# Attention with two decay kernels and a recurrent step: issuing 46 small transfers per batch from GpSimd instead of SyncE

## The reference

```
x = layernorm(x + attention(x))        # x: 16 batches x 512 tokens x 256
x = layernorm(x + ffn(x))              # a gated recurrence over the 16 batches

def attention(x):                      # 16 heads of 16
    q = heads(x @ Wq)
    out_short = softmax(q k_s^T / 4 + decay_bias) v_s     # k_s, v_s from x @ Wkv_short
    out_long  = softmax(q k_l^T / 4) v_l                  # k_l, v_l from x @ Wkv_long
    return (alpha * out_short + (1 - alpha) * out_long) @ Wo
```

## Time and profile before

| | |
|---|---|
| median of 3 executions | 2106.11 us (2104.06 to 2107.74) |
| the profiled execution: time, span | 2103.92 us, 2102.1 us |
| TensorE busy | 2015.2 us, 96% of the span |
| VectorE, ScalarE busy | 1528.0 us (73%), 1454.0 us (69%) |
| GpSimd busy | 257.6 us (12%) |
| DMAs issued by SyncE: `o_att`, `dens`, `inv_dram`, `inverses` | 512, 128, 32, 64 |
| the attention, the recurrence and the output | up to about 1750 us, from there on |

### The profile page before, as it was taken

How to read it: one execution, slowest core, us unless ns; L and a number is a source line. 1 busy time by engine, 2 the same in 40 slices (tenths; PEclk the granted TensorE clock), 3 DMA queues, 4 the chain that set the end, 5 groups by cost and what they waited for, 6 DMA issues and landing times.

```text
span 2102.1 us, 40632 instructions
## 1 busy us (share of the span) xinstructions
PE 2015.2 (96%) x15776; PEld 1059.0 (50%) x15776; DVE 1528.0 (73%) x1841; ACT 1454.0 (69%) x1750; POOL 257.6 (12%) x284
## 2 busy tenths in 40 slices
PE   6999999999999999999999999999999878999997
PEld 4444444444444444444444444444444337888887
DVE  6778888878888888888888888888887743333346
ACT  2777777777777777777777777777877663333337
POOL 0001111111111111111111101010101011000014
PEclk7999999999999999999999999999999999999999
DMA  5233333333333333333333333333323421000017
GB/s 113 65 78 78 88 79 88 80 87 80 87 80 86 80 87 81 87 80 88 80 89 79 88 81 87 80 88 78 88 70 86 112 60 35 30 30 31 31 62 260
DMA packets 157060, 170.00 MB, mean 81 GB/s; under 512 B 72756, under 2 KB 92980, under 8 KB 156868
## 3 DMA queue, kind: packets, MB, share of 16 engines
q1 hardware_dynamic: 132740, 133.61, 25.5%
q10 hardware_dynamic: 24128, 33.79, 5.2%
HBM read 54.55 MB, written 17.83 MB: 34 GB/s over the span
## 4 chain that ended last, share of the span: by engine, by line
PE 74%; ACT 8%; SPq 7%; issue 4%; DMA 3%; DVE 2%; ACTq 1%; POOL 0%; DVEq 0%; POOLq 0%
PE pv_ps L779 17%; PE pair_ps L715 13%; PE work L683 13%; PE banks L1170 13%; PE pair_ps L741 12%; ACT probs L444 7%; SPq L242 3%; PE pair_ps L691 3%; PE banks L1210 2%; DMA o_att<-pv_sb 2%; SPq L247 2%; SPq L304 1%; DVE maxes L637 1%; PE banks L1217 1%; PE banks L1163 1%
## 5 line engine op out<-in xcount | busy, mean ns | idle before, releaser
L637 DVE TENSOR_REDUCE maxes<-pair_ps 128x2 fp32r<-128x1024 f32 x1024 | 1227.9, 1221 | 262.8 <-PE pair_ps L691 147.2
L444 ACT ACTIVATE probs<-pair_ps,small 128x1024 f32<-128x1024 f32 x512 | 563.6, 1114 | 226.0 <-PE pair_ps L691 225.6
L444 ACT ACTIVATE probs<-pair_ps 128x1024 f32<-128x1024 f32 x512 | 513.6, 1024 | 123.2 <-PE pair_ps L715 111.1
L779 PE MATMUL pv_ps<-probs,vals 128*32 128x512 f32 x4096 | 548.5, 608 | 0.0
L715 PE MATMUL pair_ps<-q_op,k_op 56*128 56x512 f32 (+1 forms) x2048 | 480.6, 478 | 24.2 <-ACT probs L444 10.0
L741 PE MATMUL pair_ps<-k_op,q_op 55*128 55x512 f32 x2048 | 456.2, 442 | 24.4 <-ACT probs L444 8.0
L715 PEld LDWEIGHTS pair_ps<-q_op,k_op 56*128 56x128 f32 (+1 forms) x2048 | 192.7, 184 | 455.7 <-DVE maxes L637 201.7
L741 PEld LDWEIGHTS pair_ps<-k_op,q_op 55*128 55x128 f32 x2048 | 196.7, 187 | 201.3 <-issue 93.5
L375 POOL TENSOR_TENSOR o_att<-o_att,inverses 128x512 f32<-128x512 f32 x64 | 82.1, 1283 | 847.8 <-DMA inverses<-inv_dram 847.0
L691 PE MATMUL pair_ps<-eye_b,tri_b 64*128 64x64 bf16 x4096 | 163.8, 194 | 0.0
L691 PEld LDWEIGHTS pair_ps<-eye_b,tri_b 64*128 64x128 bf16 x4096 | 94.5, 96 | 113.4 <-issue 89.8
(11 more groups left out here) (148 smaller groups left out, 2042.6 us busy)
## 6 DMA issues: line engine op xcount, KB each, us to landing
k_op<-kq_h SPq DMA_DIRECT2D x508, 64.0 KB, 2.3
q_op<-kq_h SPq DMA_DIRECT2D x256, 64.0 KB, 2.3
o_att<-pv_sb SPq DMA_DIRECT2D x512, 32.0 KB
inverses<-inv_dram SPq DMA_DIRECT2D x64, 256.0 KB
k_op<-kq_l SPq DMA_DIRECT2D x254, 64.0 KB, 2.2
x_step<-in_xT ACTq DMA_DIRECT2D x16, 512.0 KB, 4.2
q_op<-kq_l SPq DMA_DIRECT2D x128, 64.0 KB, 2.3
q_op<-shift_rows SPq DMA_DIRECT2D x512, 2.0 KB
```

The source lines that it names most:

```text
L444: act.activation(probs[:, s % 2, 2 * hp:2 * hp + 2, :], pairs_ps[pair_of(b, s, "b", hp)][:, :, :], ACT.Exp, scale=LAM if s // 4 % 2 else 1 ...
L637: dve.reduce_max(maxima[u % 2][:, :, hp, s % 4], pairs_ps[pair_of(b, s, "a", hp)][:, :, :], mybir.AxisListType.X).then_inc(a_reduced, 1)
L779: last = pe.matmul(pv_ps[32 * h:32 * h + 32, :], vals[:, c, g // 2, att, at:at + 32], probs[:, s % 2, h, :], start=(c == 0), stop=(c == TC ...
```

## The change

`move_sums`, `store_inverses` and `load_inverses` go from `sync` to `gpsimd` with the same waits and the same transfers, and GpSimd's list is written slot by slot so that they stand among its computations. The inverses are loaded right behind their store, both at slots 3 and 19; `add_attentions` stands at slots 6 and 22, `low_part` at 9 and 25, the factors of the layer norm at 27. What GpSimd computes is the same.

```
-INVERT, STORE_INVERSES, LOAD_INVERSES, HIGH_PART = ({at: (1, -1), at + 16: (0, 0)} for at in (2, 3, 4, 9))
+INVERT, STORE_INVERSES, ADD, HIGH_PART = ({at: (1, -1), at + 16: (0, 0)} for at in (2, 3, 6, 9))
...
         def sync(sp, after):
...
                     if s % 4 == 1:
                         move_maxima(*unit_of(b, s // 4 + 1))
-                        move_sums(*sums_before(b, s // 4))
-                    for slots, move in ((STORE_INVERSES, store_inverses), (LOAD_INVERSES, load_inverses)):
-                        if s in slots:
-                            k, off = slots[s]
-                            move(b + off, k)
...
         def gpsimd(pool, after):
...
+            def move_sums(b, u):
+
+                if exists(b):
+                    g, att = u // 2, u % 2
+                    wait(pool, pv_copied, b, UNITS, u + 1)
+                    wait(pool, inv_stored, b, 16 * 2, 16 * (u // 4 - 1))
+                    pool.dma_start(dens[:, g // 2, att, g % 2, :], pv_sb[HD:P:32, att, :]).then_inc(sums_moved[att], 16)
+                    wait(pool, osum_done, b, 2, u // 4 - 1)
+                    for h in range(GH):
+                        to = HALF * (g % 2) + HD * h
+                        pool.dma_start(o_att[to:to + HD, att, g // 2, :], pv_sb[32 * h:32 * h + HD, att, :]).then_inc(sums_moved[att], 16)
...
+            def body(b):
+                for s in range(SLOTS):
+                    if s % 4 == 1:
+                        move_sums(*sums_before(b, s // 4))
+                    if s == XT_SLOT and b >= 0 and exists(b + 1):
+                        wait(pool, xt_hi, b + 1, 1, 1)
+                        pool.tensor_tensor(xt_l[(b + 1) % 2][:, :, :], xt_in, xt_h[(b + 1) % 2][:, :, :].bitcast(F32),
+                                           ALU.subtract).then_inc(xt_lo, 1)
+                    if s in STORE_INVERSES:
+                        k, off = STORE_INVERSES[s]
+                        store_inverses(b + off, k)
+                        load_inverses(b + off, k)
+                    if s in ADD:
+                        k, off = ADD[s]
+                        add_attentions(b + off, k)
+                    if s in HIGH_PART:
+                        k, off = HIGH_PART[s]
+                        low_part(b + off, k)
+                    if s == 27:
+                        factors(b - 1)
```

More of the change, by code:

```diff
@@ L292, in move_maxima @@
                         copy_words(to[:, :, at:at + 32], shift_rows[at:at + GH * TC, u % 2, :]).then_inc(shift_loaded[u % 2], 16)
[L294 to L319, removed]
             sp.wait_ge(kq_hi, 1)
@@ new lines, in store_inverses, with load_inverses @@
+            def store_inverses(b, k):
+                if exists(b):
+                    wait(pool, inverted, b, 2, k + 1)
+                    for a in range(2):
+                        wait(pool, inv_loaded[a], b, 16 * 2, 16 * (k - 1))
+                    pool.dma_start(inv_dram[k].rearrange("a g (p e) -> p (a g) e", p=P), dens[:, k, :, :, :].rearrange("p a g e -> p (a g) e")).then_inc(inv_stored, 16)
+            def load_inverses(b, k):
+                if exists(b):
+                    wait(pool, inv_stored, b, 16 * 2, 16 * (k + 1))
+                    for a in range(2):
+                        wait(pool, scaled, b, 4, 2 * k)
+                        rows = inv_dram[k, a].rearrange("g (h n) -> (g h) n", n=L)
+                        pool.dma_start(inverses[:, a, :], rows.unsqueeze(1).to_broadcast([2 * GH, HD, L])).then_inc(inv_loaded[a], 16)
@@ L375, in add_attentions @@
+            def add_attentions(b, k):
+                if exists(b):
+                    for a in range(2):
+                        wait(pool, inv_loaded[a], b, 16 * 2, 16 * (k + 1))
                         pool.tensor_tensor(o_att[:, a, k, :], o_att[:, a, k, :], inverses[:, a, :], ALU.mult).then_inc(scaled, 1)
-                    wait(pool, scaled, bb, 4, 2 * k + 2)
-                    wait(pool, done["ot"], bb, 2, k - 1)
+                    wait(pool, scaled, b, 4, 2 * k + 2)
+                    wait(pool, done["ot"], b, 2, k - 1)
@@ L378, in add_attentions, with low_part @@
                     pool.tensor_tensor(o_sum[:, k, :], o_att[:, 0, k, :], o_att[:, 1, k, :], ALU.add).then_inc(osum_done, 1)
-                def low_part(bb, k):
-                    wait(pool, ot_hi, bb, 2, k + 1)
-                    wait(pool, full["wo"], bb, 4, 0)
+            def low_part(b, k):
+                if exists(b):
+                    wait(pool, ot_hi, b, 2, k + 1)
+                    wait(pool, full["wo"], b, 4, 0)
                     pool.tensor_tensor(ot_l[:, k, :], o_sum[:, k, :], ot_h[:, k, :].bitcast(F32), ALU.subtract).then_inc(done["ot"], 1)
-                bb = b - 1
@@ L386, in body, with factors @@
[L386 to L392, removed]
+            def factors(b):
                 if exists(b):
-                    add_attentions(b, 0)
-                    low_part(b, 0)
@@ L396, in body @@
[L396 to L397 removed]
+                    wait(pool, mv_done, b, TC, TC)
                     pool.tensor_tensor(veps[:, :], mv[:, :, 1], consts[:, 0, :], ALU.add).then_inc(ln_step, 1)
[L399 removed]
+                    wait(pool, ln_step, b, 4, 3 + 1)
                     pool.tensor_tensor(rstd[:, :], veps[:, :], consts[:, 1, :], ALU.pow).then_inc(ln_step, 1)
                     pool.tensor_tensor(nmr[:, :], mv[:, :, 0], consts[:, 2, :], ALU.mult).then_inc(ln_step, 1)
[L402 removed]
+                    wait(pool, ln_step, b, 4, 3 + 3)
@@ L408, in scalar @@
+            bodies(body)
+            move_sums(B - 1, UNITS - 1)
+            store_inverses(B - 1, 1)
+            load_inverses(B - 1, 1)
+            add_attentions(B - 1, 1)
+            low_part(B - 1, 1)
+            factors(B - 1)
         def scalar(act, after):
```

7 lines of the change are left out of this document (removed).

## The result

The changed kernel takes 2092.6 us (median of 5, 2087.30 to 2095.59), the kernel before 2104.32 us in the runs beside it (median of 5, 2101.06 to 2107.74). The ratio is 0.9938, with a 95% interval of 0.9922 to 0.9954: 11.7 us faster by the medians, 13 us by the ratio. The forecast was 24.3 us slower. The rival "GpSimd issues as fast as SyncE", 13.1 us faster and 2093 us, is the case that came.

A forecast was written before the change was run, and what follows sets the result against it. TensorE's own work was taken as the bound; 11.5 + 13.0 + 3.1 - 3.3 = +24.3 us on 2103.92 us gave 2128.2, measured about 2130 us. The range was 2092 to 2200 us, leaving out about 0.15.

The forecast's parts named there:

- GpSimd issues as fast as SyncE: Rival: c about 0.6 us, no stop left at the reciprocals; 13.1 us faster, 2093 us; chance 0.25.
- What bounds the kernel: Middle batches: TensorE's own work, busy 102.9 of 105 us; the change can only touch the little that TensorE idles.
- The stop as a formula: VectorE's stop w at each reciprocal, from five issues c and landing l: w = 5c + l - 5.4, put at 2.1 us.
- l: Time from the end of the last issue of a half to the landing of its sums; rows gave 1.4 to 2.5, taken 2.0 us.
- c, the issue time on GpSimd: Time GpSimd takes to issue one DMA; no row showed it, taken as 1.1 us.
- Stops at k = 0 and k = 1: TensorE's loss behind reciprocals of the two halves: 1.3 us 16 times, +11.5 us; 0.87 us 15 times, +13.0 us.
- The end: End of the attention: last sums land 2.0 us later, store's issue +0.7, first load +0.4; together +3.1 us.
- What SyncE is rid of: SyncE's queue, 46 issues fewer a batch: nothing in middle batches, -3.3 us in the last batch's wait for maxima.
- Loads right behind the store, and GpSimd's load: GpSimd's list: waiting for the inverses costs nothing, 2.6 us to spare; GpSimd busy 65 of 104.5 us, not the bound.
- held-up issue: Rival: GpSimd's issues held up beside VectorE, c 1.86 us, w 5.9 us; +146 us, 2252 us; chance 0.13.

The follow-up runs named there:

- the slowed version: Changed kernel with a 576-column memset on GpSimd ahead of each of the five moves of a unit; 2128.46 us, ratio 1.0116 to the kernel before.
- the second profile: The changed kernel run again with no edit, beside the kernel before: 2092.62 us, ratio 0.9949.

## Why the prediction was wrong, step by step

- **What bounds the kernel.** Right. TensorE sets the batch, and what the change could touch was the 9.3 us behind the stops; it gave back 9.7 us in 15 batches. That the moves were at an edge was right too: the changed kernel's sums land an estimated 0.4 to 0.8 us ahead of the reciprocal.
- **The stop as a formula**, w = 5c + l - 5.4. Right, and shown by the slowed version: with its c = 1.06 and the l = 2.0 of the prediction it gives 5.3 + 2.0 - 5.4 = 1.9 us, and the 31 stops beside other work are 1.88 us on the mean. l was put at 2.0 and is 2.0 us on that mean (1.35 to 2.96, longer at k = 0 than at k = 1).
- **c, the issue time on GpSimd.** This is the step that failed. "What an issue resembles on this engine is an instruction whose time is not data but computing: the power over 4 columns, 1.02 us", it said, and took 1.1; measured was 0.53. The nearest row was the same instruction on another engine, SyncE's 0.59 us. The formula had its zero at c = 0.68 (with l = 2.0), between the two candidates, so that choice set the sign: w is 2.1 us by one and below zero by the other.
- **Stops at k = 0 and k = 1.** Sized +11.5 and +13.0 us for c = 1.1. With c = 0.53 both are at zero, and the 9.3 us of before come back. For the c that was assumed k = 0 was right (20.8 us in the slowed version) and k = 1 too large (8.8 us for 13.0). One reading behind it was wrong: that no idle TensorE follows a stop at k = 1. One does, in the kernel before, behind its longest stop there (timelines of VectorE and TensorE), and it puts the slack at 1.89 - 0.77 = 1.12 us, which the slowed version confirms:

```profile
1625.34 0.55 DVE L606 RECIPROCAL dens<-dens 128x64 f32<-128x64 f32 x1 [1.89 <-DMA o_att<-pv_sb]
...
1627.11 0.50 PE L715 MATMUL pair_ps<-q_op,k_op 57*128 57x512 f32 x2 [0.77 <-DVE maxes L637]
```

- **The end.** +3.1 us for c = 1.1, and the slowed version has 12.8 - 9.68 = 3.1. The total is right there and its terms are not: the reciprocal comes 1.2 us later after the copy for the 2.0 predicted, and the store's issue takes 1.70 us for 1.1. In the changed kernel the path from the last copy is 2.3 us longer (0.8 us of it in TensorE's idle time), where the rival had 0.5 us less: the store's 1.70 us and the last sums' 2.8 us to the reciprocal don't follow from c.
- **What SyncE is rid of.** Nothing in the middle, right: with SyncE as loaded as before, 8.5 us are gained all the same. In the last batch -3.3 us predicted; the wait fell by 2.25 us, and by 3.0 in the second profile, where the batch was 2.3 us shorter at the clock of before.
- **Loads right behind the store, and GpSimd's load.** Put at nothing, and TensorE waits for neither `xt_l` nor `ot_l` in the middle batches. GpSimd is busy 40.71 us of 105, not 65.
- **The rivals.** "GpSimd issues as fast as SyncE" gave 13.1 us, and its condition (c below 0.91) held. It was given 0.25. Its number came closer than its parts did: its 0.5 us for the end has the wrong sign. No "held-up issue": the longest of 512 was 536 ns, beside VectorE's reductions from first to last.

The sum had no other error of the size of c's: with nearly its own c built in, the kernel was 24 us slower, as predicted, though the k = 1 term 4 us too large and the lower clock that the sum didn't have offset each other in that total.

## What to carry to other kernels

When an engine stops at one place in each round for a transfer, ask first whether it must be there: the reciprocal one reduction later gave 8.5 us with all transfers on their queues, the whole chain one slot later 15.3, and moving 40 DMAs a batch to another engine some 12. But a consumer can be moved only as far as those behind it can wait; move the whole chain by one step, or the stop comes back elsewhere, and at a higher price where TensorE's clock falls behind it. And when a price is missing, take it from the same instruction on another engine, not from another instruction on the same engine, and if the two lie on different sides of the point of decision, give both a chance that says so.

## What the runs showed of the hardware

- GpSimd issues a DMA of 16 rows of 2 KB in 0.49 us, one of 128 rows of 2 KB in 0.62, one of 128 short runs in 0.72, in the median; SyncE took 0.59 us for the first and 0.60 for the last. Only the store to DRAM was dear, 0.85 us on the mean and 1.70 us at the end, to SyncE's 0.52 us on the median and 0.38 us at the end.
- GpSimd's arithmetic did not suffer by its own DMAs: the products over 512 columns took 1292 ns, before 1283.
- From issue to landing a move of 32 KB took 2.1 us on the median. From the end of the last issue to the reciprocal that waits for it, it was 2.8 us at the end of the attention in the changed kernel, and 1.4 us at the same place in the slowed one.
- The granted clock was 0.50, the lower level, from 532 to 540 us behind a stop of TensorE of 2.9 us, and 0.91 on the mean of the 100 us around. In the slowed version it fell behind stops of 1.72 and 2.06 us. Not every stop was followed by a fall: with the reciprocal one slot later the matmul right behind a stop of 2.57 us took 0.50 us. In that version 62 us more of idle time cost 141 us, in the slowed one 19 us more cost 26.
